# Graph transformer layer on one core: first weights and two groups' rows loaded inside the loop's block, shorter routing, route batches of 1, 1, 2, 2 and 1 groups

## The reference

```python
xn = _layernorm(x, axis=-1)
x = x + gnn(xn, edges, Wq..Wo) + mix(xn[None], w_qkv, w_out, b_out)[0]
x = x + ffn(_layernorm(x, axis=-1)[None], gate_w, gate_b, w1, b1, w2, b2)[0]
```

```python
logits = x @ gate_w + gate_b
probs = softmax(logits)
idx = argmax(probs)                  # the first of equal ones
prb = probs[idx]
pos = cumsum(one_hot(idx))[idx] - 1  # place of the row within its expert
kept = pos < C                       # C = 977
buf[idx, min(pos, C)] = x            # rows over capacity are dropped
y = (relu(buf @ w1 + b1) @ w2 + b2)[idx, pos] * (prb * kept)
```

## Time and profile before

| | |
|---|---|
| median of three runs | 2970.07 us |
| the profiled execution | 2969.6 us |
| its span, first to last instruction | 2968.4 us |
| busy, PE / PEld | 72% / 58% |
| busy, DVE | 82% |
| busy, ACT | 34% |
| busy, POOL | 71% |
| DMA | 587 MB, 198 GB/s on average |
| mean granted TensorE clock | 0.861 |

### The profile page before, as it was taken

One profiled execution on the slowest core, in us unless ns is written; L12 is line 12 of the kernel. 1 busy time (PEld: TensorE's weight loads), 2 busy tenths in 40 slices (PEclk: granted clock), 3 DMA queues, 4 the chain that ended last, 5 costly groups with the idle time before them and its releaser, 6 DMA issues. The chain is left out here.

```text
span 2968.4 us, 36266 instructions
## 1 busy us (share of the span) xinstructions
PE 2151.2 (72%) x9400; PEld 1731.9 (58%) x9401; DVE 2439.8 (82%) x3343; ACT 1010.4 (34%) x4314; POOL 2115.7 (71%) x2220
## 2 busy tenths in 40 slices
PE   5675777767777777768888876656665646499998
PEld 4573555555666665556666554444444436499998
DVE  5676778888888899999999888889999966366665
ACT  3220555555666666611111110000111004245353
POOL 4465777777777777777777777777777773667785
PEclk9796889998898999979999887787788875599999
DMA  6746777777777777778888887777777738423341
GB/s 216 246 155 172 207 211 209 208 210 220 217 218 219 219 218 219 226 233 244 259 254 258 253 238 212 211 210 211 211 211 210 211 122 282 156 68 78 86 92 15
DMA packets 257831, 587.19 MB, mean 198 GB/s; under 512 B 49411, under 2 KB 135506, under 8 KB 257566
## 3 DMA queue, kind: packets, MB, share of 16 engines
q0 software_dynamic: 150480, 467.10, 56.8%
q1 hardware_dynamic: 97947, 109.47, 11.1%
q10 hardware_dynamic: 9296, 9.44, 0.9%
HBM read 519.05 MB, written 71.76 MB: 199 GB/s over the span
## 5 line engine op out<-in xcount | busy, mean ns | idle before, releaser
L1009 POOL DMA_INDIRECT wide<-kv_d,arena x1099 | 1051.1, 956 | 334.9 <-issue 327.9
L1308 PE MATMUL ps<-wide,arena 128*128 128x264 f32 x2432 | 711.5, 456 | 230.6 <-DVE wide L1412 230.2
L1308 PEld LDWEIGHTS ps<-wide,arena 128*128 128x128 f32 x2432 | 543.4, 228 | 392.5 <-DVE wide L1412 275.8
L1009 POOL DMA_INDIRECT arena<-kv_d,arena x539 | 515.5, 956 | 164.3 <-issue 157.9
L1144 ACT ACTIVATE ps<-wide 128x256 f32 x229 | 88.8, 388 | 1317.6 <-DVE arena L1378 1275.6
L1381 DVE TENSOR_REDUCE arena<-arena 128x64 f32<-128x2048 f32 x229 | 523.5, 2286 | 7.9
L1308 PE MATMUL ps<-arena 128*128 128x264 f32 x1216 | 348.6, 449 | 125.9 <-DVE arena L1412 125.7
L1378 DVE TENSOR_TENSOR arena<-wide,ps 128x2048 f32<-128x2048 f32 x153 | 349.2, 2283 | 105.5 <-DMA wide<-kv_d,arena 105.4
L1308 PEld LDWEIGHTS ps<-arena 128*128 128x128 f32 x1216 | 266.4, 224 | 205.0 <-DVE arena L1412 149.6
L1412 DVE TENSOR_TENSOR wide<-wide,ps 128x2112 f32<-128x2112 f32 x152 | 356.7, 2347 | 26.6 <-ACT arena L1159 26.6
L140 PE MATMUL ps<-halves 128*128 128x256 f32 (+2 forms) x2304 | 361.2, 319 | 3.2 <-DVE halves L1684 1.6
(11 more groups left out here) (318 smaller groups left out, 3149.4 us busy)
## 6 DMA issues: line engine op xcount, KB each, us to landing
wide<-kv_d,arena POOLq DMA_INDIRECT x1099, 3.8
arena<-in_w SPq DMA_DIRECT2D x16, 1024.0 KB, 5.5
kv_d<-wide SPq DMA_DIRECT2D x49, 260.0 KB, 2.2
arena<-xn_d SPq DMA_DIRECT2D x82, 128.0 KB, 3.4
arena<-kv_d,arena POOLq DMA_INDIRECT x539, 3.8
...
```

The lines of the kernel that those rows point to most:

```text
L1009: e.indirect_dma_start(out=kvb[k][:, j, :], out_offset=None, in_=kv_d, in_offset=bass.IndirectOffsetOnAxis(ap=ixb[k][:, j:j + 1], axis=0)) ...
L1308: m = e.matmul(psE[(k + 1) % 3][:, 0:264], ident, kvb[b][:, j, 256:ROW], start=(j == 0), stop=(j == J - 1))
```

## The change

It has three parts.

1. SP's code inside the block gets a tail: once DVE has left the loop, load the first expert's W1 and the `base_d` rows of groups 0 and 1; once all scatters into `at_d` have landed, load the `at_d` rows of groups 0 and 1. For this the tiles stand elsewhere in `XH`: tile c at `(c + 35) % 49` ("five groups behind"), so that the first two groups lie in slots 35 to 48, behind the loop's results which fill the front of `wide` until they are scattered. The loads of groups 2 to 6 stay behind the block; the weights no longer follow them.
2. `route` is shorter. The maximum of the logits is found as the zeros of the shifted logits instead of by comparing probabilities with their maximum; the gate's probability is the reciprocal of the sum of exponentials, as the largest exponential is 1; the slot base comes from the expert's number in the same operation as the position; the scan's mask is made once; the last conversion to an integer is part of the last addition. The exponential on ACT is emitted one step later, and the matmuls in a piece of their own with the sum and the reciprocal behind them.
3. The batches of groups change from 2, 2, 1, 1, 1 to 1, 1, 2, 2, 1.

```diff
@@ -22,7 +22,8 @@
...
-BATCHES = ((0, 2), (2, 4), (4, 5), (5, 6), (6, 7))
+BATCHES = ((0, 1), (1, 2), (2, 4), (4, 6), (6, 7))
+AHEAD = 35
@@ -871,6 +872,27 @@
...
+        XH = R12[:, 0:NT * XW].rearrange("p (t w) -> p t w", w=XW)
+        s_x2 = [sem(f"s_x2_{i}") for i in range(7)]
+        s_we = [sem("s_we0"), sem("s_we1")]
...
+        t_x2 = {}
+
+        def place(c):
+            return (c + AHEAD) % NT
+
+        def tiles_of(grp):
+            return slice(place(7 * grp), place(7 * grp) + 7)
+
+        def attention_in(grp):
+            t_x2[grp] = dma(Y, XH[:, tiles_of(grp), 0:256], at_d[grp * 896:grp * 896 + 896, :].rearrange("(t p) d -> p t d", p=128), s_x2[grp])
+
+        def base_in(grp):
+            n_, r0, c0 = (7 if grp < 6 else 6), grp * 896 + 128, place(7 * grp)
+            t_x2[grp] = dma(Y, XH[:, c0:c0 + n_, 256:512], base_d[r0:r0 + 128 * n_, :].rearrange("(t p) d -> p t d", p=128), s_x2[grp])
+            if grp == 6:
+                t_x2[grp] = dma(Y, XH[:, place(48), 256:512], base_d[0:128, :], s_x2[grp])
+
@@ -988,6 +1010,16 @@
...
+            e.wait_ge(sv.h, sv.n + 2)
+            for k in range(RING):
+                e.wait_ge(e_bs[k], 16 * (AUX + (k == RING - 1)))
+            s_we[0].inc(e.dma_start(w1r, kpart(w1[0])), 16)
+            base_in(0)
+            base_in(1)
+            e.wait_ge(s_ag.h, 16 * NT)
+            attention_in(0)
+            attention_in(1)
@@ -1491,34 +1523,33 @@
...
-        XH = R12[:, 0:NT * XW].rearrange("p (t w) -> p t w", w=XW)
+        wait(Y, t_fin, t_ag)
+        for grp in range(2, 7):
+            attention_in(grp)
+            base_in(grp)
+
...
-        for k in range(RING):
-            Y.wait_ge(e_bs[k], 16 * (AUX + (k == RING - 1)))
-        wait(Y, t_fin, t_ag)
-        t_x2, t_sum = {}, {}
-        for grp in range(7):
-            n_ = 7 if grp < 6 else 6
-            c0, r0 = grp * 7, grp * 896
-            rows_of = lambda d, r: d[r:r + 128 * n_, :].rearrange("(t p) d -> p t d", p=128)
-            dma(Y, XH[:, c0:c0 + 7, 0:256], at_d[r0:r0 + 896, :].rearrange("(t p) d -> p t d", p=128), s_x2[grp])
-            t_x2[grp] = dma(Y, XH[:, c0:c0 + n_, 256:512], rows_of(base_d, r0 + 128), s_x2[grp])
-        t_x2[6] = dma(Y, XH[:, 48, 256:512], base_d[0:128, :], s_x2[6])
...
+        reset = R3[:, 3951:3951 + 184]
+        resets = {7: reset[:, 0:64].rearrange("p (e c) -> p e c", e=8), 14: reset[:, 64:184].rearrange("p (e c) -> p e c", e=8)}
+        void = R3[:, 4400:4401]
+        t_sum = {}
...
-        v(V.tensor_scalar(out=off8, in0=iota[:, 0:8], scalar1=float(CP), scalar2=None, op0=ALU.mult))
         v(V.memset(carry, 0.0))
         t_k = v(V.memset(reset, 1.0))
-        wait(V, t_k, t_ag)
-        t_k = v(V.tensor_copy(XH[:, :, 512].bitcast(i32), tokid[:, 0:NT]))
+        wait(V, t_k)
+        for z in resets.values():
+            v(V.memset(z[:, :, 0], 0.0))
+        v(V.tensor_scalar(out=void, in0=valid, scalar1=-16384.0, scalar2=16384.0, op0=ALU.mult, op1=ALU.add))
+        wait(V, t_ag)
+        v(V.tensor_copy(XH[:, AHEAD:NT, 512].bitcast(i32), tokid[:, 0:NT - AHEAD]))
+        t_k = v(V.tensor_copy(XH[:, 0:AHEAD, 512].bitcast(i32), tokid[:, NT - AHEAD:NT]))
@@ -1559,57 +1590,47 @@
...
-            rs_ = reset[:, 0:8 * (n + 1)].rearrange("p (e c) -> p e c", e=8)
             ce = lambda z: z.rearrange("p e c -> p c e")
             wait(V, t_ld[g1 - 1])
             seq(V.tensor_reduce(col(mx), l, AX.X, ALU.max))
             t = v(V.tensor_tensor(l, l, bc(mx), ALU.subtract))
+            yield
             wait(S, t)
-            t = a(S.activation(ex, l, ACT.Exp))
-            yield
-            v(V.memset(reset, 1.0))
+            t_ex = a(S.activation(ex, l, ACT.Exp))
             wait(V, (sv, sv.n))
-            v(V.memset(rs_[:, :, 0], 0.0))
             v(V.tensor_copy(oh[:, :, 0], carry))
-            wait(V, t)
-            seq(V.tensor_reduce(col(sm), ex, AX.X, ALU.add))
-            seq(V.reciprocal(col(sm), col(sm)))
-            yield
-            seq(V.tensor_tensor(ex, ex, bc(sm), ALU.mult))
-            seq(V.tensor_reduce(col(pm), ex, AX.X, ALU.max))
-            v(V.tensor_copy(XH[:, c0:c1, 513], col(pm)))
-            seq(V.tensor_tensor(q_, ex, bc(pm), ALU.is_equal))
-            seq(V.tensor_tensor(q_, q_, rowe(rev), ALU.mult))
+            seq(V.scalar_tensor_tensor(out=q_, in0=l, scalar=0.0, in1=rowe(rev), op0=ALU.is_equal, op1=ALU.mult))
             seq(V.tensor_reduce(col(wv), q_, AX.X, ALU.max))
             seq(V.tensor_tensor(ce(oh[:, :, 1:n + 1]), bc(wv), rowe(rev), ALU.is_equal))
             if c1 == NT:
                 seq(V.tensor_scalar(out=oh[:, :, n], in0=oh[:, :, n], scalar1=valid, scalar2=None, op0=ALU.mult))
-            t = v(V.tensor_tensor_scan(pre_[:, 0:8 * (n + 1)], reset[:, 0:8 * (n + 1)], ohs[:, 0:8 * (n + 1)], 0.0, ALU.mult, ALU.add))
+            t = v(V.tensor_tensor_scan(pre_[:, 0:8 * (n + 1)], reset[:, 64 * (n > 7):64 * (n > 7) + 8 * (n + 1)], ohs[:, 0:8 * (n + 1)],
+                                       0.0, ALU.mult, ALU.add))
+            yield
             wait(T, t, t_rt[0])
             b = ps[3][:, 64:512]
             T.matmul(b[:, 0:8 * n], ones, pr[:, :, 0:n], start=True, stop=False)
             tm = sp.inc(T.matmul(b[:, 0:8 * n], tri, oh[:, :, 1:n + 1], start=False, stop=True))
             wait(V, t)
             v(V.tensor_copy(carry, pr[:, :, n]))
-            seq(V.tensor_tensor(q_, ce(oh[:, :, 1:n + 1]), rowe(off8), ALU.mult))
-            seq(V.tensor_reduce(col(bs), q_, AX.X, ALU.add))
+            wait(V, t_ex)
+            seq(V.tensor_reduce(col(sm), ex, AX.X, ALU.add))
+            p0 = place(c0)
+            v(V.reciprocal(XH[:, p0:p0 + n, 513], col(sm)))
             yield
             wait(V, tm)
             t_rt[0] = v(V.tensor_tensor(q_, ce(b[:, 0:8 * n].rearrange("p (e c) -> p e c", e=8)), ce(oh[:, :, 1:n + 1]), ALU.mult))
             wait(V, t_rt[0])
             seq(V.tensor_reduce(col(pos), q_, AX.X, ALU.add))
-            seq(V.tensor_scalar(out=col(kept), in0=col(pos), scalar1=float(C), scalar2=None, op0=ALU.is_lt))
+            seq(V.tensor_scalar(out=col(kept), in0=col(pos), scalar1=float(C), scalar2=16384.0, op0=ALU.is_ge, op1=ALU.mult))
             if c1 == NT:
-                seq(V.tensor_scalar(out=kept[:, 48:49], in0=kept[:, 48:49], scalar1=valid, scalar2=None, op0=ALU.mult))
-
-            seq(V.tensor_scalar(out=col(kept), in0=col(kept), scalar1=-16384.0, scalar2=16384.0, op0=ALU.mult, op1=ALU.add))
-            seq(V.tensor_tensor(col(pos), col(pos), col(kept), ALU.add))
-            seq(V.tensor_tensor(col(pos), col(pos), col(bs), ALU.add))
-            t_sl = v(V.tensor_copy(slotS[:, c0:c1], col(pos)))
+                seq(V.tensor_scalar(out=kept[:, 48:49], in0=kept[:, 48:49], scalar1=void, scalar2=None, op0=ALU.max))
+            seq(V.scalar_tensor_tensor(out=col(pos), in0=col(wv), scalar=-float(CP), in1=col(pos), op0=ALU.mult, op1=ALU.add))
+            t_sl = v(V.scalar_tensor_tensor(out=slotS[:, c0:c1], in0=col(pos), scalar=float(H * CP), in1=col(kept), op0=ALU.add, op1=ALU.add))
             wait(G, t_sl, t_hz)
...
-                                                  in_=XH[:, c, 256:XW], in_offset=None, bounds_check=H * CP - 1, oob_is_err=False), 16)
+                                                  in_=XH[:, place(c), 256:XW], in_offset=None, bounds_check=H * CP - 1, oob_is_err=False), 16)
@@ -1626,11 +1647,11 @@
...
-            part = XH[:, grp * 7:grp * 7 + 7, :]
+            part = XH[:, tiles_of(grp), :]
@@ -1693,8 +1712,7 @@
...
-        wait(Y, t_fin)
-        load_w(0, 0)
+        t_wl[0][0] = (s_we[0], s_we[0].n)
         wait(G, t_fin)
         split_w(0, 0)
```

More of the change, by code:

```diff
@@ L872, in gps_layer_kernel @@
         l_fin, l_tp, l_at, l_wo, l_ao, l_sc = [esem(n) for n in ("lfin", "ltp", "lat", "lwo", "lao", "lsc")]
+        XH = R12[:, 0:NT * XW].rearrange("p (t w) -> p t w", w=XW)
+        s_x2 = [sem(f"s_x2_{i}") for i in range(7)]
+        s_we = [sem("s_we0"), sem("s_we1")]
+        w1r, w2r = r3(R0[:, 0:2048], 1024), r3(R0[:, 2048:4096], 256)
+        t_x2 = {}
[10 more added lines that the diff above has]
+                t_x2[grp] = dma(Y, XH[:, place(48), 256:512], base_d[0:128, :], s_x2[grp])
         loop = ExitStack()
@@ L1498, in gps_layer_kernel @@
         ohs, pre_ = R3[:, 2048:2048 + 456], R3[:, 2560:2560 + 456]
-        mx, sm, pm, wv, pos, kept, bs = [R3[:, 3584 + 49 * i:3633 + 49 * i] for i in range(7)]
-        rev, off8, carry = [R3[:, 3927 + 8 * i:3935 + 8 * i] for i in range(3)]
-        reset = R3[:, 3951:3951 + 456]
-        s_x2 = [sem(f"s_x2_{i}") for i in range(7)]
-        for k in range(RING):
-            Y.wait_ge(e_bs[k], 16 * (AUX + (k == RING - 1)))
-        wait(Y, t_fin, t_ag)
-        t_x2, t_sum = {}, {}
-        for grp in range(7):
-            n_ = 7 if grp < 6 else 6
-            c0, r0 = grp * 7, grp * 896
```

(24 more changed lines are left out.)

## The result

| | before | changed |
|---|---|---|
| median of 6 runs | 2968.32 us | 2950.11 us |
| lowest to highest | 2967.89 to 2970.16 | 2948.30 to 2952.31 |
| profiled execution, its span | 2969.57, 2968.4 | 2950.27, 2949.1 |

The ratio is 0.9936, with a 95% interval of 0.9926 to 0.9946: 18.2 us less by the medians. The forecast was 2952, worked out as 18.0 us less than the 2970.07 of the first three runs.

The account below looks back on a forecast made before the run. Bound: the last scatter, held by POOL's 49.31 us weights wait. With the change, block opening, VectorE through group 3 and 35 scatters end at 2554.3 against 2572.27; 2970.07 less 18.0 gives 2952, range 2945 to 2960.

Parts of the forecast that it names:

- Weights in the block: At the block's opening: POOL splits from 2455.0, its 49.31 us wait goes, and slot supply becomes the limit.
- Rows in the block: VectorE's first sum, group 0: rows are in by 2456.7, so it starts at 2456.35, 6.56 us earlier.
- Routing: VectorE and PE between sums: shorter routes give periods of 10.66 us with 7 columns, 11.14 with 14, 8.22 without.
- rival C: At the group periods: stalls vanish, all periods are 8.22 us, sum of group 5 4.9 us sooner; 2947, chance 0.07.
- VectorE beside the split: Sums of groups 0 and 1 beside POOL's split: 0.44 us longer each, 0.9 us added.
- the 1.8 us: Sums beside POOL's split: by the skill's exclusion rule each could wait a whole 0.91 us subtraction, 1.8 instead of 0.9.
- From slots to scatter: Between VectorE's slots of groups 2 and 3 and POOL's first of the last scatters: 0.1 us.
- The 35 scatters: POOL's last run: starts at 2509.5, 34 steps of 1.3175 us, ends at 2554.3 against 2572.27, 18.0 us earlier.
- The experts: Behind the last scatter: read-back, transposes and experts are unchanged and shift as a whole.
- A: At the block's close: the barrier holds because SP has transfers in flight, +7.8 us, 2960; chance 0.12.
- B: At the routes: shorter on VectorE, but PE and ScalarE do not profit; 6.1 us lost, 2958; chance 0.08.
- D: POOL's scatters starve beside row loads and stores: 2.56 us a step, 42 us more, 2994; chance 0.03.

Follow-up runs that it names:

- e7: Changed kernel with the first expert's W1 loaded behind all rows, as before; on a slower chip, ratio 0.9979 to the kernel before, gain 9.0 us.
- e4: Changed kernel with all rows loaded behind the block, as before; on a slower chip, ratio 0.9938 to the kernel before, gain 23.2 us.
- e6: Changed kernel with the old routing code, new batches and loads; on a slower chip, ratio 0.9939 to the kernel before, gain 20.9 us.
- e9: Changed kernel again without any edit, on a slower chip; 3371.01 us, ratio 0.9913 to the kernel before, gain 29.4 us.

## Why the prediction was right, step by step

- **Weights in the block.** Right in place and reason: POOL splits with the opening, the wait went over to VectorE's slots, and e7 brings the old wait back.
- **Rows in the block.** Foreseen 1.38 us behind the opening, measured 0.81: the prelude took 0.81 us for 0.98 before, where it was to grow by 0.4. The rows were in time. e4 gives the price of leaving them out, 7.4 us at the first sum, and on the chip of the result that sum came 7.13 us earlier, where 6.56 were foreseen.
- **Routing.** The periods were to be 10.66, 10.66, 8.22 and 11.14; they are 10.65, 10.71, 8.21 and 11.16. e6 measures 1.8 us for each small route. The sum of old rows less the operations taken out was right because PE's wait for the scan stays in its row (1.55 and 1.85 us), which rival C denied.
- **VectorE beside the split.** 0.9 us assumed, 0.24 measured: from the first sum to the third it is 12.96 us, against 12.72; one sum took 2.23 for 2.02. The term was mis-sized, and its row misread. The sum at 2505.15, 2.46 us, had no scatter beside it, as the first starts at 2509.03; it lay beside the subtractions of the split. But the sum at 2460.13, beside the subtractions of the changed kernel, took 2.01 us, so they didn't make the 0.44. What recurs is the sum beside the casts: 2.22 us at 2496.93 before, 2.23 at 2454.15 now. e7, where no split lies beside it, has 2.02 us for that sum and 12.73 from the first sum to the third, against 2.23 and 12.96 in e9. Nor is there a whole subtraction's wait on either side, as the 1.8 us would have it: the eight subtractions took 7.38 us for 7.31.
- **From slots to scatter.** 0.1 us assumed, 0.80 measured (2506.52 to 2507.32; 0.82 at the first batch, 2476.27 to 2477.09). This error is more than made up by the first sum and by VectorE beside the split, which came out 0.6 and 0.7 better than assumed. That the end agrees to 0.3 us is in part luck; the terms alone are good to 0.7.
- **The 35 scatters.** 34 steps were to take 44.8 us and took 45.0, without a gap. The last one stands 98.98 us behind the opening, 117.30 before: 18.3 us gained, 18.0 foreseen. The path is as foreseen: block open, VectorE through group 3, 35 scatters, read-back.
- **The experts** shift as a whole but for 0.67 us in the first products, within the 1.4 us by which that stretch varies over the profiles. So −1.63 (loop) − 18.3 + 0.67 = −19.3, the difference of the profiled executions, and without the loop's share −17.7 against −18.2 by the medians.
- **Rivals.** A: SP's DRAIN takes 0.12 us and the opening follows the start of the loop's last scatter by 8.4 in each kernel, with row loads in flight (e9) or without (e4). B: the short periods refute it. C: the waits stayed. D: 4 of 49 scatters were long (2.12 to 2.75 us), one of them among the 35; the mean step there is 1.32, far from 1.85.

What stays open: what the pauses on the slower chips wait for, why the gain there is larger and how it divides, and whether old or single batches would do better on the chip of the result. On that chip the parts weren't taken back one at a time; there the account rests on the two profiles.
